# Token loop of a fused mixture-of-experts, two-attention and FFN kernel: layer two's values and layer one's context ahead of both value halves

## The chip, the cores and the metric

One core of a Trainium2 chip runs the whole program. The metric is the device time in microseconds; the time before is the median of three runs. TensorE (PE) does the matmuls, with its weight loads (PEld) running beside them; VectorE (DVE), ScalarE (ACT), GpSimd (POOL) and SyncE (SP) each work through a queue of their own in the order in which the kernel writes them, and wait for one another by semaphores.

## The reference

A residual block over 32 sequences of 64 tokens with 256 channels:

```
x = x + attn1(experts(x, cond))          # 8 experts, top 2; 16 heads of 64, tanh projections, causal
x = x + ffn(attn2(x, cond))              # 16 heads of 16, coherence gate and field term; FP4 rounding

attn1: q, k, v = tanh(s @ W + b);  p = softmax(mask(q k^T / 8));  tanh((p v) @ Wo + bo)
attn2: q, k, v = x @ Wqkv^T + b;   mod = softmax(q k^T / 4) * coh / sum;
       mod = 0.79 * mod + 0.21 * field;  (mod v) @ Wout^T + bout
```

The weights come in float32 and so do nearly all matmuls; the FP4-rounded product at the end is done in bfloat16 parts.

## The kernel before

**Stages.** The program first computes the gate, sorts the token slots by expert and runs the experts over 128-row tiles (up to some 320 us). Then a token loop takes the 2048 tokens as TT = 16 tiles of 128 tokens, two sequences each, through both attention layers and the FFN. The order of the work is written out by hand, one list of steps for each engine, and the loop is pipelined over tiles: in TensorE's turn t (lines 1080 to 1112) layer one works on tile t (projections, values, scores) and on tile t-1 (turning the probabilities, context, output projection), layer two on tile t-2 (projections, scores, values) and on tile t-3 (context, output, FFN). VectorE's list (lines 1916 to 1942) is the same pipeline with its index one higher: its turn t+1 serves TensorE's turn t.

**TensorE's steps around the change.** After the key projections of tile t come
- `l2_scores(t - 2)` (line 983, matmuls at L993): all heads' scores of layer two into banks 4 to 7;
- `l1_v(t, 0)` (line 860, L869): the values of the first sequence of tile t, 8 matmuls, into bank 3;
- `l1_context(t - 1)` (line 908, L919): layer one's context into banks 1 and 2;
- `l1_v(t, 1)`: the values of the second sequence, into bank 0;
- `l2_v(t - 2)` (line 971, L978): layer two's values into bank 6. It waits until both subtractions on VectorE have read the scores, which lie in banks 4 to 7:

```
pe.wait_ge(u2_set, 2 * t + 2)
```

- `l1_scores(t)` (line 874, L887): layer one's scores into banks 3 and 0, which hold the value halves until then, so it waits for both value biases (`vb_set`);
- `l2_turn_q(t - 3)` (L1033) and `l1_out(t - 1)` (line 923, L928), the output projection, which waits for the two context copies.

The value halves are called value half 0 and 1 below. `tail_busy` puts small matmuls on bank 0 in single turns after the last tile.

**VectorE's steps around the change.** `l2_max` (line 1829, L1834) takes the row maxima of layer two's scores in two halves, `l2_shift` (line 1836, L1840) subtracts them, in two halves, and each subtraction releases one exponential of 512 columns on ScalarE (`l2_exp`, L1323). `l1_v(t, s)` (line 1752, L1758) adds the value bias to a half and moves it from PSUM to `v`; for half 0 it also waits for the context of the tile before, since that reads `v`:

```
dve.wait_ge(v_ps, 2 * t + s + 1)
if t and s == 0:
    dve.wait_ge(ctx_ps, t)
```

`l1_ctx` (line 1778, L1783) copies the context out of PSUM, in two halves. `l2_sums` (line 1850, L1854 to L1857) are four instructions, the row sums of both exponentials and what is made of them. `l2_v` (line 1815, L1824) adds layer two's value bias, two instructions, after `v2_ps`. `l2_share` (line 1859, L1862) then scales the exponentials. Later in the turn come the mask (L1765), the bias of the output projection (L1790) and more.

**Other queues.** GpSimd gathers the expert outputs of a coming tile, SyncE loads x and stores the result; ScalarE does tanh, exponentials and copies out of PSUM in its own list (from line 1361).

Of the kernel before, what the change touches and what calls it, by code (L numbers as in the profile page):

```python
# [30 lines left out]
TT = TOK // P  # L31
# [64 lines left out]
def exists(t, n):  # L96

    return not isinstance(t, int) or 0 <= t < n
# [12 lines left out]
def value_bank(t, s):  # L111

    return (1, 2)[s] if t == 0 else (3, 0)[s]
# [46 lines left out]
def build(nc, t_in, out):  # L160
    ctx = ExitStack()
    with ctx:
# [453 lines left out]
        def _(pe):  # L616
# [205 lines left out]
            def halves():  # L822

                return [(s, slice(s * SEQ, (s + 1) * SEQ)) for s in range(2)]

            def l1_turn_m(t):
                if not exists(t, TT):
                    return
                pe.wait_ge(m_set, t + 1)
                if t > 1:  # L830
                    pe.wait_ge(exp1_set, 2 * t)
                elif t == 0:
                    pe.wait_ge(h1t_set, SLOT_TILES)
                for k in range(KH):
                    last = pe.transpose(ps[:, turn_bank(t), k * P:(k + 1) * P], m_rows[:, k * P:(k + 1) * P], ident[:, :])
                last.then_inc(mt_ps, 1)
# [23 lines left out]
            def l1_v(t, s):  # L860
                if not exists(t, TT):
                    return
                if t:
                    pe.wait_ge(qk_set, 4 * t + 3 + s)
                if t == 1:
                    pe.wait_ge(exp1_set, 1 + s)
                for k in range(KH):
                    for r in range(2):
                        last = mm(ps[r * SEQ:(r + 1) * SEQ, value_bank(t, s), :], m_t[:, k, s * SEQ:(s + 1) * SEQ],  # L869
                                  wv[:, k, r * 512:(r + 1) * 512], start=k == 0, stop=k == KH - 1,  # L870
                                  tile_position=(0, r * SEQ))
                last.then_inc(v_ps, 1)
# [35 lines left out]
            def l1_context(t):  # L908
                if not exists(t, TT):
                    return  # L910
                pe.wait_ge(pt1_set, 2 * t + 2)
                pe.wait_ge(v_set, t + 1)
                for cm in range(4):
                    for s, q in halves():
                        for r in range(2):
                            rows_ = slice(r * SEQ, (r + 1) * SEQ)
                            for g in range(2):
                                at, h = cm * P + s * SEQ, 2 * cm + g
                                last = mm(ps[g * D1:(g + 1) * D1, 1 + r, at:at + SEQ], v[rows_, s, h * D1:(h + 1) * D1],  # L919
                                          pt1[rows_, 4 * g + cm, q], start=True, stop=True, tile_position=(r * SEQ, g * D1))  # L920
                last.then_inc(ctx_ps, 1)
# [49 lines left out]
            def l2_v(t):  # L971
                if not exists(t, TT):
                    return
                pe.wait_ge(u2_set, 2 * t + 2)
                for s, q in halves():
                    for k in range(KH):
                        for r in range(2):
                            last = mm(ps[r * SEQ:(r + 1) * SEQ, 6, s * P:(s + 1) * P], x1_t[:, k, q],  # L978
                                      wv2[:, k, r * P:(r + 1) * P], start=k == 0, stop=k == KH - 1,
                                      tile_position=(0, r * SEQ))  # L980
                last.then_inc(v2_ps, 1)
# [54 lines left out]
            def l2_ffn(t):  # L1036
                if not exists(t, TT):
                    return
                pe.wait_ge(xqt_set, t + 1)
                for k in range(KH):  # L1040
                    for n in range(PARTS):
                        last = mm(bank(7, HID), xq_t[:, k, :], wffn[:, k, n, :], start=k + n == 0,
                                  stop=(k, n) == (KH - 1, PARTS - 1))
                last.then_inc(f_ps, 1)

            def tail_busy(t, last, n):
                if t == last:
                    for _ in range(n):
                        mm(bank(0, P), ident_h[:, :], ident_h[:, :], start=True, stop=True)
# [30 lines left out]
            for t in range(2, TT + 4):  # L1080
                l1_turn_m(t)
                l2_ffn(t - 4)
                tail_busy(t, TT + 2, 20)
                l2_turn_p(t - 3, 0)
                l1_q(t, 0)
                l2_turn_p(t - 3, 1)
                l1_turn_x1(t - 2)
                l1_q(t, 1)
                l2_hidden(t - 2)
                l2_context(t - 3)  # L1090
                l1_k(t, 0)
                l2_coherence(t - 2)
                l2_out(t - 3)
                l2_q_or_k(t - 2, 4, wq2)
                l1_turn_p(t - 1, 0)
                l2_q_or_k(t - 2, 5, wk2)
                l1_k(t, 1)
                l1_turn_p(t - 1, 1)
                tail_busy(t, TT, 14)
                tail_busy(t, TT + 1, 20)  # L1100
                l2_scores(t - 2)
                l1_v(t, 0)
                tail_busy(t, TT, 12)
                l1_context(t - 1)
                l1_v(t, 1)
                tail_busy(t, TT, 10)
                tail_busy(t, TT + 1, 44)
                l2_v(t - 2)
                l1_scores(t)
                tail_busy(t, TT + 2, 70)  # L1110
                l2_turn_q(t - 3)
                l1_out(t - 1)
# [272 lines left out]
        def _(dve):  # L1385
# [366 lines left out]
            def l1_v(t, s):  # L1752
                if not exists(t, TT):
                    return
# [3 lines that stand above are left out]
                tt(v[:, s, :], bank(value_bank(t, s)), half_row("bv"), ALU.add).then_inc(vb_set, 1)  # L1758
# [19 lines left out]
            def l1_ctx(t, n):  # L1778
                if not exists(t, TT):
                    return  # L1780
                if n == 0:
                    dve.wait_ge(ctx_ps, t + 1)
                dve.tensor_copy(ctx_t[:, 4 * n:4 * n + 4, :], ps[:, 1 + n, :].rearrange("p (c q) -> p c q", c=4)  # L1783
                                ).then_inc(ctx_set, 1)
# [30 lines left out]
            def l2_v(t):  # L1815
                if not exists(t, TT):
                    return
                if t == 0:
                    dve.wait_ge(v2_zeroed, 1)
                dve.wait_ge(v2_ps, t + 1)  # L1820
                for s in range(2):
                    dst = v2[:, s, :, :].rearrange("p (g o) (w d) -> p g (o w) d", o=2, w=2)[:, :, 0::3, :]
                    src = lambda ap: ap.rearrange("p (g o d) -> p g o d", o=2, d=D2)
                    last = tt(dst, src(ps[:, 6, s * P:(s + 1) * P]), src(half_row("bv2")), ALU.add)  # L1824
                    last.then_inc(v2_set, 1)
# [24 lines left out]
            def l2_sums(t):  # L1850
                if not exists(t, TT):
                    return
                dve.wait_ge(exp2_set, 2 * t + 2)
                step(red(z2, u2, X, ALU.add))  # L1854
                step(stt(r2, coh, MOD_EPS, z2, ALU.add, ALU.mult))
                step(dve.reciprocal(r2, r2))
                step(stt(r2, coh, 1.0 - FI, r2, ALU.mult, ALU.mult))  # L1857
# [58 lines left out]
            for t in range(3, TT + 4):  # L1916
                l1_mix(t)
                l1_mask(t - 2, 1)
                l2_field(t - 4, 1)
                l1_sums(t - 2)  # L1920
                l1_share(t - 2)
                l2_bias_a(t - 4)
                l2_z(t - 3)
                l2_scales(t - 4)
                l2_coherence(t - 3)
                l2_round(t - 4)
                l2_max(t - 3, 0)
                l2_max(t - 3, 1)
                l2_shift(t - 3, 0)
                l1_v(t - 1, 0)  # L1930
                l2_shift(t - 3, 1)
                l1_ctx(t - 2, 0)
                l1_v(t - 1, 1)
                l1_ctx(t - 2, 1)
                l2_sums(t - 3)
                l2_v(t - 3)
                l2_share(t - 3)
                l1_mask(t - 1, 0)
                l1_bias_o(t - 2)
                l2_result(t - 4)  # L1940
                l2_x1_bias(t - 3)
                l1_residual(t - 2)
                l2_field(t - 3, 0)
# [72 lines left out]
```

## Time and profile before

| | |
|---|---|
| median of three runs | 769.49 us (768.01 to 771.59) |
| the profiled execution's own time | 771.83 us |
| its span in the trace | 770.1 us |
| granted clock of TensorE, mean | 0.986 |
| token loop at its full length, in the trace | 395 to 714 us |

Times in the trace are microseconds from the start of the span. "Idle before" is the time that an engine stood idle ahead of an instruction, with what released it ("<-"); a releaser of "issue" means that the profile shows nothing that was waited for. The ends of matmuls are modelled, and neighbouring matmuls overlap in the timeline; in the chain of waits the pieces are laid end to end. Some matmul records are missing (a piece of 64 is listed as x53).

### The profile page before, as it was taken

The numbers are of one execution on the slowest core, as the hardware profiler recorded it, in microseconds if no ns is written. First come the engines' busy times: TensorE is split into PE (matmuls) and PEld (weight loads), VectorE is DVE, ScalarE is ACT, GpSimd is POOL, SyncE is SP. The second block draws the span as 40 slices with busy tenths as digits, with TensorE's granted clock in tenths as the row PEclk, the third lists the DMA queues.
The fourth block names the chain that finished last, engine by engine and source line by source line (L and its number), as shares of the span: only waits on it lengthen the run. The fifth ranks groups of instructions, "written<-read, shape, count | busy, mean of one in ns | idle before, by whom it ended". The sixth has DMA issues, their size and how long they took to land.

```text
span 770.1 us, 22516 instructions
## 1 busy us (share of the span) xinstructions
PE 729.0 (95%) x9300; PEld 629.2 (82%) x9300; DVE 499.1 (65%) x1100; ACT 282.3 (37%) x823; POOL 87.9 (11%) x93
## 2 busy tenths in 40 slices
PE   5389999999999999989999999999999999999986
PEld 2279999569999999868888888897888889888775
DVE  3846564744454444244787778778777877877975
ACT  3032211141212212245445544544553555455331
POOL 2131112411111100111100110111011001000000
PEclk9599999999999999999999999999999999999999
DMA  7687411217111103200000010010010001000000
GB/s 261 259 328 264 152 35 52 81 48 254 42 35 36 38 19 111 90 29 22 22 17 15 29 30 9 23 29 23 9 30 29 16 16 29 17 2 16 16 9 14
DMA packets 20113, 49.26 MB, mean 64 GB/s; under 512 B 3051, under 2 KB 14699, under 8 KB 18477
## 3 DMA queue, kind: packets, MB, share of 16 engines
q1 hardware_dynamic: 10960, 32.47, 11.6%
q0 software_dynamic: 3744, 10.49, 4.7%
q10 hardware_dynamic: 5309, 4.87, 1.9%
q8 instruction: 74, 1.21, 0.7%
q14 instruction: 26, 0.21, 0.1%
HBM read 41.00 MB, written 6.82 MB: 62 GB/s over the span
## 4 chain that ended last, share of the span: by engine, by line
PE 90%; DVE 5%; ACT 2%; issue 1%; DMA 1%; another core or an unknown queue 0%; DVEq 0%; ACTq 0%; SPq 0%
PE ps L843 15%; PE ps L742 15%; PE ps L712 8%; PE ps L869 8%; PE ps L928 7%; PE ps L776 7%; PE ps L944 3%; PE ps L894 3%; PE ps L887 2%; PE ps L919 2%; PE ps L1025 2%; PE ps L959 2%; PE ps L1015 2%; PE ps L978 2%; PE ps L993 2%; PE ps L736 1%
## 5 line engine op out<-in xcount | busy, mean ns | idle before, releaser
L843 PE MATMUL ps<-arena,l_weights 128*128 128x128 f32 x1024 | 125.9, 277 | 2.1 <-issue 1.7
L742 PE MATMUL ps<-h_t,w_now 128*128 128x128 f32 x1056 | 123.5, 275 | 1.7 <-DVE h_t L1614 1.1
L843 PEld LDWEIGHTS ps<-arena,l_weights 128*128 128x128 f32 x1024 | 119.3, 192 | 4.1 <-issue 1.8
L742 PEld LDWEIGHTS ps<-h_t,w_now 128*128 128x128 f32 x1056 | 120.5, 192 | 2.1 <-issue 2.1
L1167 ACT ACTIVATE h_t<-ps,cols 128x128 f32<-128x128 f32 x132 | 37.6, 367 | 166.6 <-PE ps L712 144.4
L1589 DVE COPY w_now<-arena 128x2048 f32 x33 | 40.5, 1227 | 81.8 <-PE ps L742 75.3
L1240 ACT ACTIVATE arena<-ps,cols 128x128 f32<-128x128 f32 x256 | 73.6, 382 | 52.0 <-PE ps L843 52.0
L607 POOL DMA_INDIRECT arena<-expert_out,slot_of x32 | 32.7, 1023 | 333.9 <-DVE arena L1642 286.8
L712 PEld LDWEIGHTS ps<-xg_t,w_now 128*128 128x128 f32 x528 | 63.4, 192 | 5.7 <-issue 3.5
L712 PE MATMUL ps<-xg_t,w_now 128*128 128x128 f32 x528 | 65.0, 276 | 2.7 <-ACT h_t L1167 2.2
L576 POOL DMA_INDIRECT xg<-in_x,slot_tok x36 | 42.2, 1174 | 190.5 <-PE ps L691 159.2
L776 PE MATMUL ps<-arena,h_t 128*128 x264 | 62.5, 379 | 0.0
L869 PE MATMUL ps<-l_weights,arena 128*64 128x512 f32 x256 | 61.8, 604 | 0.0
L928 PE MATMUL ps<-l_weights,arena 128*128 128x256 f32 x256 | 58.9, 383 | 0.0
L928 PEld LDWEIGHTS ps<-l_weights,arena 128*128 128x128 f32 x256 | 47.4, 190 | 5.9
L776 PEld LDWEIGHTS ps<-arena,h_t 128*128 128x128 f32 x264 | 47.6, 190 | 5.1
L1574 DVE COPY w_now<-arena 128x1024 f32 x33 | 23.1, 701 | 31.4 <-PE ps L712 23.6
L1614 DVE TENSOR_SCALAR h_t<-ps,cols 128x128 f32<-128x128 f32 x132 | 37.0, 343 | 4.7 <-PE ps L742 4.6
L894 PE MATMUL ps<-ident,arena 128*128 128x128 f32 x256 | 38.4, 273 | 0.8 <-DVE arena L1862 0.6
L1758 DVE TENSOR_TENSOR arena<-ps,half_rows 128x512 f32<-128x512 f32 x32 | 22.0, 687 | 25.4 <-PE ps L919 19.9
L1878 DVE TENSOR_TENSOR arena<-ps,rows 128x256 f32<-128x256 f32 x16 | 6.8, 425 | 45.1 <-PE ps L1025 45.0
L1323 ACT ACTIVATE arena<-arena 128x512 f32<-128x512 f32 x32 | 20.1, 631 | 38.6 <-DVE arena L1840 38.6
(302 smaller groups left out, 1116.6 us busy)
## 6 DMA issues: line engine op xcount, KB each, us to landing
arena<-in_experts SPq DMA_DIRECT2D x8, 2048.0 KB
expert_out<-y ACTq DMA_DIRECT2D x36, 128.0 KB
arena<-in_x_t SPq DMA_DIRECT2D x2, 1024.0 KB, 7.5
arena<-in_x SPq DMA_DIRECT2D x16, 128.0 KB
out<-arena SPq DMA_DIRECT2D x16, 128.0 KB, 1.7
b<-in_b SPq DMA_DIRECT2D x1, 1024.0 KB, 5.0
l_weights<-in_wq SPq DMA_DIRECT2D x1, 1024.0 KB
l_weights<-in_wk SPq DMA_DIRECT2D x1, 1024.0 KB
```

The costliest lines, as they stand in the source:

```text
L576: pool.indirect_dma_start(out=xg[j % XG][:, :], out_offset=None, in_=t_in["x"], in_offset=bass.IndirectOffsetOnAxis(ap=slot_tok[:, slot_ti ...
L712: last = mm(ps[:, 0, m * P:(m + 1) * P], w1_now[:, k, m * P:(m + 1) * P], xg_t[:, k, :], start=k == 0, stop=k == KH - 1)
L742: last = mm(ps[:, 2, m * P:(m + 1) * P], w2_now[:, k, m * P:(m + 1) * P], h1_t[j % 2][:, k, :], start=k == 0, stop=k == KM - 1)
L776: last = mm(bank(4, HID), h2_t[j % 2][:, k, :], flat[:, bass.ds(at + k * HID, HID)], start=k == 0, stop=k == KM - 1)
L843: last = mm(ps[:, b, c * P:(c + 1) * P], wt[:, k, f:f + P], m_t[:, k, :], start=k == 0, stop=k == KH - 1)
L869: last = mm(ps[r * SEQ:(r + 1) * SEQ, value_bank(t, s), :], m_t[:, k, s * SEQ:(s + 1) * SEQ], wv[:, k, r * 512:(r + 1) * 512], start=k == ...
L894: last = pe.transpose(bank_[:, m * P:(m + 1) * P], p[:, h:h + 2, :], ident[:, :])
L928: last = mm(bank(1, HID), ctx_t[:, c, :], wo[:, c, :], start=c == 0, stop=c == C1 - 1)
L1167: last = f(h1_t[j % 2][:, k, :], ps[:, 0, k * P:(k + 1) * P], ACT.Relu, bias=cols[:, bass.ds(e * KM + at + k, 1)])
L1240: last = f(dst[:, cc, :], ps[:, project_bank(t, n), c * P:(c + 1) * P], ACT.Tanh, bias=col(bias)[:, cc:cc + 1])
L1589: dve.tensor_copy(w2_now[:, :, :].rearrange("p k n -> p (k n)"), arena[:, bass.ds(at, KM * MID)]).then_inc(w2_set, 1)
L1614: last = ts(h2_t[j % 2][:, k, :], ps[:, 2, k * P:(k + 1) * P], cols[:, bass.ds(e * KM + at + k, 1)], 0.0, ALU.add, ALU.max)
```

## The change

On TensorE, for the turns with t < 16, layer two's values move from behind the second value half to directly behind layer two's scores, and both value halves come after layer one's context, one behind the other. In later turns the order stays. On VectorE the bias of value half 0 leaves its place between the two subtractions; the two context copies and layer two's value biases come next, then the bias of half 0, the sums of layer two, and the bias of half 1.

```diff
@@ TensorE, turn t
                 l2_scores(t - 2)
-                l1_v(t, 0)
+                if t < TT:
+                    l2_v(t - 2)
                 tail_busy(t, TT, 12)
                 l1_context(t - 1)
+                l1_v(t, 0)
                 l1_v(t, 1)
-                tail_busy(t, TT, 10)
-                tail_busy(t, TT + 1, 44)
-                l2_v(t - 2)
+                if t >= TT:
+                    tail_busy(t, TT, 10)
+                    tail_busy(t, TT + 1, 44)
+                    l2_v(t - 2)
                 l1_scores(t)
@@ VectorE, turn t
                 l2_shift(t - 3, 0)
-                l1_v(t - 1, 0)
                 l2_shift(t - 3, 1)
                 l1_ctx(t - 2, 0)
+                l1_ctx(t - 2, 1)
+                l2_v(t - 3)
+                l1_v(t - 1, 0)
+                l2_sums(t - 3)
                 l1_v(t - 1, 1)
-                l1_ctx(t - 2, 1)
-                l2_sums(t - 3)
-                l2_v(t - 3)
                 l2_share(t - 3)
```

## Rows read from the trace of the kernel before

**Rows 1.** The page, part 1: engine, busy us, share of the span, instructions.

```profile
PE 729.0 (95%) x9300; PEld 629.2 (82%) x9300; DVE 499.1 (65%) x1100; ACT 282.3 (37%) x823; POOL 87.9 (11%) x93
```

**Rows 2.** Busy time by stretch, the full token loop: PE, PEld, DVE, ACT, POOL; clock, DMA, GB/s.

```profile
395.24:714.05 318.81, 318.74 (x5137) 270.30 (x5137) 248.62 (x527) 160.75 (x469) 20.97 (x20) 1.00 0.07 20
```

**Rows 3.** Chain of waits, start and length: L928 in turns 3 and 15.

```profile
395.24 3.51 PE ps L928 x16
...
714.05 3.51 PE ps L928 x16
```

**Rows 4.** Chain of waits, the changed stretch of turn 7.

```profile
493.82 0.84 PE ps L993 x53
494.66 1.87 PE ps L869 x8
496.53 1.09 PE ps L919 x64
497.62 1.87 PE ps L869 x8
499.49 0.87 PE ps L978 x16
```

**Rows 5.** Timeline of VectorE, the same stretch: start, length, instruction, idle before.

```profile
494.70 1.42 DVE L1834 TENSOR_REDUCE arena<-ps 128x8 f32<-128x512 f32 x2 [0.18 <-PE ps L993]
496.15 0.69 DVE L1840 TENSOR_TENSOR arena<-ps,arena 128x512 f32<-128x512 f32 x1
497.76 0.69 DVE L1758 TENSOR_TENSOR arena<-ps,half_rows 128x512 f32<-128x512 f32 x1 [0.92 <-PE ps L919]
498.37 0.68 DVE L1840 TENSOR_TENSOR arena<-ps,arena 128x512 f32<-128x512 f32 x1
498.96 0.68 DVE L1783 COPY arena<-ps 128x512 f32<-128x512 f32 x1
499.56 0.68 DVE L1758 TENSOR_TENSOR arena<-ps,half_rows 128x512 f32<-128x512 f32 x1
...
500.76 1.21 DVE L1854 TENSOR_REDUCE arena<-arena 128x16 f32<-128x1024 f32 x1
...
502.71 0.49 DVE L1824 TENSOR_TENSOR arena<-ps,half_rows 128x128 f32<-128x128 f32 x2
```

**Rows 6.** Timeline of the other engines, the same stretch.

```profile
499.08 0.63 ACT L1323 ACTIVATE arena<-arena 128x512 f32<-128x512 f32 x1 [1.58 <-DVE arena L1840]
499.10 1.02 PEld L978 LDWEIGHTS ps<-arena 128*64 128x64 f32 x16 [0.50 <-DVE arena L1840]
499.32 1.04 PE L978 MATMUL ps<-arena 128*64 128x128 f32 x16
...
500.30 1.02 PEld L887 LDWEIGHTS ps<-arena 64*64 64x64 f32 x64 [0.18 <-DVE arena L1758]
```

**Rows 7.** Timeline of the tail, turn 17.

```profile
752.28 1.09 PE L978 MATMUL ps<-arena 128*64 128x128 f32 x16 [1.01 <-DVE arena L1840]
752.92 1.22 DVE L1854 TENSOR_REDUCE arena<-arena 128x16 f32<-128x1024 f32 x1 [0.70 <-ACT arena L1323]
...
753.31 0.28 PE L1033 MATMUL ps<-before,arena 128*128 128x128 bf16 x2
...
754.88 0.49 DVE L1824 TENSOR_TENSOR arena<-ps,half_rows 128x128 f32<-128x128 f32 x2
755.29 1.22 DVE L1862 TENSOR_TENSOR arena<-arena 128x1024 f32<-128x1024 f32 x1
```

**Rows 8.** TensorE's idle times in the setup, and the clock by stretch.

```profile
7.86 1.93 PE L633 MATMUL ps<-arena 128*32 128x512 f32 x8 [3.48 <-DMA arena<-in_x_t]
...
21.82 0.29 PE L664 MATMUL ps<-maskb,before 128*128 128x128 bf16 x1 [5.71 <-DVE maskb L1465]
...
4.00:8.00 4.00, 0.52 (x8) 0.35 (x10) 1.87 (x12) 0.26 (x1) 1.26 (x5) 1.00 1.00 416
...
16.00:20.00 4.00, 0.10 (x1) 0.00 (x0) 3.41 (x14) 1.39 (x2) 0.00 (x0) 0.85 1.00 428
```

## Prediction, made before the change was run

> **What bounds the kernel now.** I began with the page's busy table: TensorE is busy for 95% of the span, VectorE for 65% [rows 1]. A share is an average, so the next view was the busy time of the stretch in which the token loop runs at its full length, 395.24 to 714.05 us: TensorE 318.74 of 318.81 us, granted clock 1.00, VectorE 248.62 [rows 2]. There TensorE has no idle time that anything could take away. The chain of waits gives the length of a turn: the attention output projection (L928) starts at 395.24 in one turn and at 714.05 twelve turns later [rows 3], 318.81 / 12 = 26.57 us a turn. So in this loop every wait of TensorE's queue, which runs in the written order, is new time, and no wait of another engine costs anything until TensorE stands behind it.
>
> Then I read one turn's chain from layer two's scores to layer one's scores [rows 4]. Scores of layer two end at 493.82 + 0.84 = 494.66; then value half 0 (1.87), context (1.09), value half 1 (1.87), layer two's values (0.87), done at 500.36, when layer one's scores follow. All the pieces touch. VectorE's timeline of the same stretch [rows 5] shows what these pieces cover: the two maxima start 0.04 after the scores, the first subtraction at 496.15, but the second only at 498.37, since the bias of value half 0 stands ahead of it and waits 0.92 for the context. Layer two's values on TensorE (L978) wait for the second subtraction: its weight load begins at 499.10, 0.05 after 498.37 + 0.68, while value half 1 is still streaming [rows 6]. The cover is just long enough. Layer one's scores (L887) wait for the bias of value half 1, which ends at 499.56 + 0.68 = 500.24; the load begins at 500.30 [rows 6]. That one is hidden by layer two's values.
>
> **The change part by part.** The work is the same, instruction for instruction: nothing is added or removed, no DMA moves, SP, POOL and ScalarE keep their order. Only what covers what changes, in the 14 turns t = 2 to 15 in which all the pieces exist.
>
> *Layer two's values directly behind layer two's scores (TensorE).* They write bank 6, which holds scores until both subtractions have read it, so l2_v waits for them, with only l2_scores ahead. That is a loop through VectorE that nothing can cover: maxima 494.70 + 1.42 = 496.12, first subtraction at 496.15, the second 0.60 later (the step between the PSUM readers of rows 5, as 498.37 to 498.96), 496.75 + 0.68 = 497.43, plus 0.05 to TensorE = 497.48. Queued behind the wait are the context, both value halves, layer one's scores and everything after. TensorE stands still 497.48 - 494.66 = **2.82 us**. The move on VectorE (bias of half 0 out from between the subtractions) is counted here: with the bias left there, each queue would wait for the other; so it is a condition of the first move and no saving on top.
>
> *What follows on TensorE.* Layer two's values, now from a standing start: in the tail they do this already, begun at 752.28 behind a wait, and the next piece begins at 753.31 [rows 7], so 1.03, done at 498.51. The low bound is the 0.87 of rows 4. Context 1.09: 499.60. Value halves 1.87 each: 501.47 and 503.34. Their inputs are ready: the pieces now come later than they did.
>
> *VectorE's order behind the subtractions.* Context copies wait for the context: 499.60 + 0.14 (before, the context ends at 496.53 + 1.09 = 497.62 and the bias starts at 497.76; the hand-over ahead of the maxima is 0.04) = 499.74, and the second 0.60 later, 500.34. Layer two's value biases from 500.94, 0.41 for both (754.88 to 755.29, [rows 7]): 501.35. Bias of half 0 waits for 501.47 + 0.14 = 501.61. Now **the piece the title does not mention**: l2_sums stands between the two biases. It needs the second exponential of layer two, 0.63 on ScalarE after the subtraction [rows 6], so about 498.2: ready. It starts 0.60 after the bias, 502.21, and its four instructions last 500.76 to 502.71 = 1.95 [rows 5], so 504.16. Bias of half 1: 504.16 to 504.85, although its product is there at 503.34. Layer one's scores may load at 504.85 + 0.06 = **504.91**; before, the load began at 500.30. TensorE's second stand is 504.91 - 503.34 = 1.57.
>
> *Per turn*: 504.91 - 500.30 = 4.61 (as a check: stands 2.82 + 1.57, restart 0.16, 0.06 from the pieces' start points). Times 14 = **64.5 us**. Bounds per turn: 4.2 (values at 0.87, no delay in the hand-overs) and 5.2 (each of the two restarts pays once more the 0.22 between load and first product, 499.10 to 499.32 in rows 6), so 59 to 73 us.
>
> *Who else is late.* Between layer one's scores and the next l2_scores both queues are unchanged. VectorE comes earlier to the attention shares of layer two (they follow the bias of half 1 directly; before, 2.8 after the score load), ScalarE's exponentials follow the scores as before, and VectorE waited for TensorE just ahead of the maxima. I cost all that at nothing; its cover is the 3.51 us of L928 [rows 3].
>
> *Tail, t = 16 and on.* The guard leaves TensorE's order as it was. VectorE takes layer two's value biases ahead of its sums there too. At t = 17 the sums started at 752.92; now the biases wait for L978, which ends at 753.37, so start 753.5, end 753.9, sums to 753.9 + 1.96 (752.92 to 754.88) = 755.9 against a share start of 755.29 [rows 7]: **+0.6 us**, on the chain. At t = 16 the projection covers the same delay: 0, bounded by the same 0.6.
>
> **Sum.** 64.5 + 0.6 = 65.1 us; 771.83 of the profiled execution (its span is 770.1) gives 836.9. That execution lies 2.3 above the median of the runs, 769.49, so on the median I forecast 834.6.
>
> **The clock.** A stand in every turn could cost clock. The rows: TensorE idle for 3.48 us ahead of the gate's products kept the granted clock at 1.00 (2.4 GHz) in 4 to 8 us; idle for 5.71 it shows 0.85 in 16 to 20 [rows 8]. The stands of 2.82 and 1.57 with 5.9 us of work between are shorter than the one that cost nothing. I take no loss.
> [...]
>
> **Rivals.**
> (a) *The clock falls in each turn.* For it: two stands a turn, 14 times, where rows 2 has none. Against it: rows 8. Price: if 4 us after a stand run at 1.2 GHz, 2 us of work are lost per turn, 28 us: 863.
> (b) *The second stand is shorter.* If the bias of half 1 were not behind the sums, it would end at 503.34 + 0.14 + 0.69 = 504.17 and the load begin at 504.23: 3.93 a turn, 55 + 0.6 us, 825. Only if sums finish before value half 1 does, that is if VectorE gains 0.7 us on rows 5. The order written in the diff speaks against.
> (c) *Faster.* The loop is really bound by the ring through VectorE (context, bias of half 0, second subtraction, values), and TensorE's records, whose ends are modelled, only look dense. Place: the 0.92 us wait ahead of the bias of half 0 [rows 5]; it goes. 14 x 0.92 = 12.9 us: 756.6. It decides only if TensorE could run its 5.7 us between the two scores in under 4.8; that the same pieces have the same length in every turn and load early (rows 6) speaks against.
> (d) *No change*: the two value halves side by side would have to save 4.6 us a turn, but last 3.74 together [rows 4]. Excluded as a single cause.
>
> **How the numbers follow.** Forecast 0.85 (834.6, own range 828 to 843 from the bounds 59 to 73); (b) 0.06; (a) 0.06, of which part is a smaller loss between the two; (c) 0.02; (d) 0.01. The range 825 to 848 takes in (b) and a partial (a), and leaves out the full (a), (c), (d). A measurement of this kernel can tell about 0.5% from no change: slower 0.97, same 0.01, faster 0.02.
>
> **What would show it.** Right: turn length 31.2 us between starts of L928; TensorE idle ahead of L978 of about 2.8 us with the second subtraction named as releaser, 14 times, and ahead of L887 of about 1.6 with the value bias named; the second subtraction 0.60 behind the first; the bias of half 1 directly behind the sums; granted clock 1.00 through the loop. Wrong: no idle ahead of L978, or a granted clock under 1.00 in the loop with matmuls of double length (a), or the idle ahead of L887 under 1 us (b), or new idle ahead of other lines than these two.

## The result, and the profile after

The changed kernel takes 860.03 us (median of six runs, 855.16 to 861.96) against 769.97 us of the kernel before (six runs): a ratio of 1.1165, with a 95% interval of 1.1132 to 1.1197. That is slower, as forecast, but by 90.1 us where 65.1 were forecast, and outside the range of 825 to 848. One of the four executions of the kernel with only its second stand filled (below) was in a slow state, 1192.71 us at a mean clock of 0.619; its ratio leaves that one out, and its median would be 851.01 without it.

A stand is, here as in the prediction, a stretch in which TensorE has nothing to do because the head of its queue waits.

The page of the profiled execution (span 853.4 us), busy time, the slices of TensorE and its granted clock, and a group of part 5:

```profile
PE 751.6 (88%) x9300; PEld 643.4 (75%) x9300; DVE 501.6 (59%) x1100; ACT 281.9 (33%) x823; POOL 87.9 (10%) x93
...
PE   4499999999999999897897897897988978978886
...
PEclk8699999999999999999999898999988999989999
...
L978 PE MATMUL ps<-arena 128*64 128x128 f32 x256 | 24.6, 353 | 40.7 <-DVE arena L1843 40.7
```

Two things differ from [rows 1]. TensorE's share fell from 95 to 88%, and its busy time rose, 729.0 to 751.6, with the same 9300 matmuls. A wait cannot do the second. The clock's row gives it away: 8 in several slices of the loop, where the kernel before has 9 throughout. (The changed kernel's VectorE lines are three higher: L1840 is L1843, L1834 L1837, L1758 L1761, L1783 L1786, L1824 L1827, L1854 L1857, L1862 L1865.)

Busy time of the twelve turns 4 to 15, from L928 to L928 as in [rows 2]:

```profile
400.56:796.78 396.22, 342.60 (x5138) 285.37 (x5137) 250.81 (x526) 160.33 (x468) 20.96 (x20) 0.93 0.06 16
```

396.22 / 12 = 33.0 us a turn against 26.57. TensorE is idle for 53.6 us of it, 4.47 a turn; and it is busy for 342.60 instead of 318.74, 23.9 us more, at a mean clock of 0.93.

The first stretch below is turn 3, which ran at full clock, the second turn 7, the turn of [rows 4] (timeline of TensorE: start, length, instruction, idle before):

```profile
391.94 1.09 PE L978 MATMUL ps<-arena 128*64 128x128 f32 x16 [2.83 <-DVE arena L1843]
392.96 1.16 PE L919 MATMUL ps<-arena 64*64 64x64 f32 x64
394.06 3.65 PE L869 MATMUL ps<-l_weights,arena 128*64 128x512 f32 x16
399.35 1.16 PE L887 MATMUL ps<-arena 64*64 64x64 f32 x64 [1.64 <-DVE arena L1761]
...
520.82 1.98 PE L978 MATMUL ps<-arena 128*64 128x128 f32 x16 [2.83 <-DVE arena L1843]
522.73 1.99 PE L919 MATMUL ps<-arena 64*64 64x64 f32 x64
524.64 4.83 PE L869 MATMUL ps<-l_weights,arena 128*64 128x512 f32 x16
531.11 1.16 PE L887 MATMUL ps<-arena 64*64 64x64 f32 x64 [1.63 <-DVE arena L1761]
```

Both stands are there, 2.83 and 1.64 us, in either turn. In turn 7 the work behind the first stand also takes longer, 1.98 for 1.09, 1.99 for 1.16 and 4.83 for 3.65. The clock over the same turn (columns as in [rows 2]; the stretches are the stand, the values with the context, the value halves, the second stand):

```profile
517.90:520.82 2.92, 0.09 (x9) 0.00 (x1) 2.67 (x4) 2.13 (x7) 0.00 (x0) 0.90 0.00 0
520.82:524.64 3.82, 3.82 (x80) 3.37 (x80) 0.00 (x0) 0.61 (x2) 0.00 (x0) 0.50 0.02 4
524.64:529.47 4.83, 4.83 (x20) 1.33 (x16) 3.35 (x6) 0.00 (x0) 0.00 (x0) 0.75 0.00 0
529.47:531.10 1.63, 0.00 (x1) 0.00 (x0) 1.49 (x6) 0.00 (x0) 0.00 (x0) 1.00 0.00 0
```

The granted clock falls to 0.50 (1.2 GHz) some 0.6 us before the stand ends (a mean of 0.90 over its 2.92 us), and returns to 1.00 (2.4 GHz) in the middle of the value halves. The fall does not always come inside the stand. In turn 5 the stand and layer two's values behind it (454.21 to 455.31) still have 1.00, and the clock falls as the context begins:

```profile
455.31:457.08 1.77, 1.77 (x65) 1.65 (x65) 0.00 (x0) 0.00 (x0) 0.00 (x0) 0.52 0.03 9
```

VectorE's timeline of turn 7, to set beside [rows 5]:

```profile
518.03 1.42 DVE L1837 TENSOR_REDUCE arena<-ps 128x8 f32<-128x512 f32 x2 [0.17 <-PE ps L993]
519.48 1.29 DVE L1843 TENSOR_TENSOR arena<-ps,arena 128x512 f32<-128x512 f32 x2
524.78 1.29 DVE L1786 COPY arena<-ps 128x512 f32<-128x512 f32 x2 [4.02 <-PE ps L919]
525.99 0.48 DVE L1827 TENSOR_TENSOR arena<-ps,half_rows 128x128 f32<-128x128 f32 x2
527.80 0.69 DVE L1761 TENSOR_TENSOR arena<-ps,half_rows 128x512 f32<-128x512 f32 x1 [1.34 <-PE ps L869]
528.41 1.21 DVE L1857 TENSOR_REDUCE arena<-arena 128x16 f32<-128x1024 f32 x1
...
530.36 0.69 DVE L1761 TENSOR_TENSOR arena<-ps,half_rows 128x512 f32<-128x512 f32 x1
```

The subtractions follow each other at once, and the sums stand between the two biases, as read off the diff.

**Where the 90 us went.** The starts of L928 give each turn's length. At full clock turn 4 is 31.13 us against 26.60 before, so the waits are 4.53 a turn; the first two turns give 4.67 and 4.60. Over 14 turns that is 4.67 + 4.60 + 12 x 4.53 = 63.6 us. From L928 of turn 1 to L928 of turn 15 the two traces differ by 455.10 - 368.43 = 86.7 us, which leaves 23.1 us. All of it lies in the 11 turns from 5 on, which are 32.4 to 34.0 us long: one fall costs from 1.2 to 2.9 us. The tail is 0.4 longer (56.62 against 56.21). The stretch ahead of the loop, which the change does not touch, was 3.8 us shorter in this execution: 86.7 + 0.4 - 3.8 = 83.3, the difference of the two spans. The medians differ by more, 90.1, also because this execution of the changed kernel was the fastest of its six (855.16 us at a mean clock of 0.955; the two slowest, 861.89 and 861.96, had 0.945).

### The profile page after: what moved, and what is told of

Its sections match the earlier page's. It is cut to its first block, busy times and chain, and to the rows that moved or that the text cites. A ratio compares the mean times of both kernels' runs of the same rounds, so it can differ in the third digit from the quotient of the medians.

```text
span 853.4 us, 22515 instructions
## 1 busy us (share of the span) xinstructions
PE 751.6 (88%) x9300; PEld 643.4 (75%) x9300; DVE 501.6 (59%) x1100; ACT 281.9 (33%) x823; POOL 87.9 (10%) x93
## 4 chain that ended last, share of the span: by engine, by line
PE 80%; DVE 15%; issue 2%; ACT 1%; DMA 1%; DVEq 1%; another core or an unknown queue 0%; SPq 0%; ACTq 0%
PE ps L843 14%; PE ps L742 13%; PE ps L712 7%; PE ps L928 7%; PE ps L776 6%; PE ps L869 5%; PE ps L944 3%; PE ps L919 3%; PE ps L894 3%; PE ps L978 3%; DVE arena L1837 2%; DVE arena L1761 2%; DVE arena L1843 2%; PE ps L887 2%; DVE arena L1857 2%; PE ps L1025 2%
## 5 line engine op out<-in xcount | busy, mean ns | idle before, releaser
L712 PE MATMUL ps<-xg_t,w_now 128*128 128x128 f32 x528 | 65.1, 276 | 2.9 <-ACT h_t L1170 2.2
L869 PE MATMUL ps<-l_weights,arena 128*64 128x512 f32 x256 | 66.9, 668 | 0.0
L1265 ACT ACTIVATE arena<-ps 128x512 f32<-128x512 f32 x32 | 19.0, 605 | 144.5 <-PE ps L887 144.5
L978 PE MATMUL ps<-arena 128*64 128x128 f32 x256 | 24.6, 353 | 40.7 <-DVE arena L1843 40.7
L928 PE MATMUL ps<-l_weights,arena 128*128 128x256 f32 x256 | 58.9, 383 | 0.0
L928 PEld LDWEIGHTS ps<-l_weights,arena 128*128 128x128 f32 x256 | 47.4, 190 | 5.9
L978 PEld LDWEIGHTS ps<-arena 128*64 128x64 f32 x256 | 19.4, 180 | 42.9 <-DVE arena L1843 42.8
L1786 DVE COPY arena<-ps 128x512 f32<-128x512 f32 x32 | 20.7, 685 | 47.1 <-PE ps L919 47.1
L869 PEld LDWEIGHTS ps<-l_weights,arena 128*64 128x64 f32 x256 | 18.7, 154 | 34.9 <-issue 33.3
L887 PEld LDWEIGHTS ps<-arena 64*64 64x64 f32 x1024 | 16.4, 134 | 37.7 <-DVE arena L1761 36.9
```

The lines of the kernel that those rows point to most:

```text
L712: last = mm(ps[:, 0, m * P:(m + 1) * P], w1_now[:, k, m * P:(m + 1) * P], xg_t[:, k, :], start=k == 0, stop=k == KH - 1)
L887: last = mm(slot(S1, 8 * g + 2 * cm + r)[q, :], q_t[rows_, c, q], k_t[rows_, c, q], start=True, stop=True, tile_position=(g * D1, s * SEQ))
L928: last = mm(bank(1, HID), ctx_t[:, c, :], wo[:, c, :], start=c == 0, stop=c == C1 - 1)
```

## The experiments

Each time stands beside runs of the kernel before in the same series on the same chip, since that kernel itself took 766 us in some series and 770 to 771 in others, and both on one chip. The edits are to the changed kernel, with two exceptions: the seven matmuls ahead of the context go into the kernel with the context first, and in the last section the edit is to the kernel with the values moved back. In the kernels with `fill` the lines of ScalarE and VectorE lie eleven higher than in the changed kernel: L1854 is there the subtraction (L1843) and L1772 the value bias (L1761).

### Filling the stands

`fill(t, b, n)` issues n matmuls `mm(bank(b, P), ident_h, ident_h)` in bfloat16, whose product nobody reads; the work of the kernel is unchanged. The first line below fills the first stand, the second line the second; each of the three kernels has the one, the other or both.

```diff
                 l2_scores(t - 2)
+                fill(t, 3, 40)
                 if t < TT:
                     l2_v(t - 2)
...
+                fill(t, 5, 22)
                 l1_scores(t)
```

The first stand alone:

> Forty small bfloat16 matmuls on bank 3 (free since the tanh of the first key half) stand between layer two's scores and layer two's values in every turn; nothing else differs from the changed kernel. The small matmuls fill about 2.4 us of the first stand of 2.83 us and add nothing to it. Theory A (the two stands cost 4.6 us a turn, and the rest of the loss, about 25 us of 90, is the clock that falls because TensorE is idle in the first stand): the granted clock is 1.00 through the loop, layer two's values, the context and the value halves take 1.09, 1.16 and 3.65 us in every turn, and the time is about 770 + 65 = 835 us. Rival B (those pieces are slow because VectorE and ScalarE work on PSUM beside them, or for another reason tied to the new order): they stay at up to 1.98, 1.99 and 4.83 us in most turns, and the time stays at 860.

Measured: 835.35 against 770.80 us, 1.0838 (1.0791 to 1.0884), so 64.6 us more. One turn of it (L1059 are the small matmuls), and twelve turns:

```profile
484.76 2.41 PE L1059 MATMUL ps<-before 128*128 128x128 bf16 x40
487.65 1.09 PE L978 MATMUL ps<-arena 128*64 128x128 f32 x16 [0.49 <-DVE arena L1854]
488.68 1.16 PE L919 MATMUL ps<-arena 64*64 64x64 f32 x64
489.77 3.65 PE L869 MATMUL ps<-l_weights,arena 128*64 128x512 f32 x16
495.06 1.16 PE L887 MATMUL ps<-arena 64*64 64x64 f32 x64 [1.63 <-DVE arena L1772]
...
402.84:776.07 373.23, 347.70 (x5618) 297.14 (x5617) 250.75 (x526) 160.35 (x468) 20.97 (x20) 1.00 0.06 18
```

The waits are as long as they were, 2.41 + 0.49 = 2.90 with the small matmuls in them; the clock is 1.00, the pieces have their full-speed length in all 14 turns, and 25.5 of the 90.1 us are gone (two series, each against its own runs of the kernel before). TensorE did more work and the kernel became faster than the changed one. Theory A held, rival B fell.

Both stands:

> As before this one, with 22 more small matmuls on bank 5 ahead of layer one's scores, which fill about 1.3 us of the second stand of 1.64 us. Theory A with the first stand alone as the cause of the clock's fall: the same time as with the first stand filled, 835 us. Theory A2 (both stands together matter): 835 here, but between 840 and 860 with only the first filled. Rival B: 860 in both.

835.13 against 770.80 us, 1.0830 (1.0801 to 1.0859): no different.

The second stand alone:

> The changed kernel with the 22 small matmuls on bank 5 ahead of layer one's scores alone: the second stand is filled, the first of 2.83 us is bare. Theory A (the first stand alone makes the clock fall): falls in most turns as in the changed kernel, 855 to 860 us. Rival A2 (the two stands only do it together): granted clock 1.00 and 835 us.

851.26 against 766.65 us, 1.1087 (1.1060 to 1.1114), so 84.6 more. The first stand stays at 2.83, and the clock falls in every one of the 14 turns; a turn is 32.3 to 32.5 us. So the first stand is enough to make the clock fall, and the second takes no part that filling it could remove. A fall costs less here, some 1.3 us (32.3 to 32.5 against 31.1 a turn with both stands filled): 14 falls are some 19 us against 23 for the changed kernel's 11, which is most of the 5 us beneath it.

Half of the first stand, 20 small matmuls:

> The changed kernel with 20 small matmuls in place of 40 in the first stand, so that about 1.7 us of it are idle. If the length of one idle stretch decides, this is like the stand of the kernel with the context first (1.23 behind 0.44), whose clock fell in every second turn: a value between 835 and 860, about 845. If what decides is idle time summed over both stands, it is worse than that. If 1.7 us are short enough: 835.

830.81 against 766.65 us, 1.0835 (1.0813 to 1.0858), so 64.2 more. Idle ahead of L978 is 1.61 us (1.68 in the first), the clock 1.00 in all. Neither 845 nor worse: this much idle time in one piece cost no clock, although the second stand of 1.63 us follows in each turn.

### One part of VectorE's order undone

```diff
                 l1_v(t - 1, 0)
-                l2_sums(t - 3)
                 l1_v(t - 1, 1)
+                l2_sums(t - 3)
```

> The changed kernel, but on VectorE the bias of value half 1 stands ahead of layer two's sums. Theory A: the second stand falls from 1.64 to about 0.9 us (0.14 + 0.69 + 0.06), the first stays at 2.83 and the clock goes on falling as in the changed kernel, so 14 x 0.74 = 10 us less, 850 us. If the second stand had a part in the clock's fall, less than 847. Rival C (the second stand is set by something else, such as the two value halves' own end): it stays at 1.64 and the time at 860.

849.12 against 770.80 us, 1.1024 (1.0991 to 1.1058): 78.3 more, so 11.7 less than the changed kernel. In the turn below, at a low clock, VectorE waits for the value halves ahead of both biases instead of doing the sums; the idle time of TensorE ahead of L887 is 0.8 us in all turns, and the clock falls in 13 of 14.

```profile
495.64 0.69 DVE L1761 TENSOR_TENSOR arena<-ps,half_rows 128x512 f32<-128x512 f32 x1 [1.19 <-PE ps L869]
497.35 0.69 DVE L1761 TENSOR_TENSOR arena<-ps,half_rows 128x512 f32<-128x512 f32 x1 [1.02 <-PE ps L869]
497.96 1.21 DVE L1857 TENSOR_REDUCE arena<-arena 128x16 f32<-128x1024 f32 x1
```

So the sums between the biases cost 0.84 us a turn, which the title of the change doesn't mention. Rival C fell.

### The context ahead of layer two's values

```diff
-                if t < TT:
-                    l2_v(t - 2)
                 tail_busy(t, TT, 12)
                 l1_context(t - 1)
+                if t < TT:
+                    l2_v(t - 2)
```

> The changed kernel, but TensorE does layer one's context between layer two's scores and layer two's values, so that the first stand shrinks to 2.83 - 1.09 = 1.74 us. VectorE's copies follow the subtractions at once. The bias of half 1 then ends some 1.1 us earlier: 3.5 us more a turn than the kernel before. Theory A with a clock that does not fall at stands this short: 770 + 49 = 819 us and a granted clock of 1.00. If it falls all the same: up to 844.

826.04 against 770.80 us, 1.0710 (1.0646 to 1.0775), so 55.2 more, between the two cases. One turn:

```profile
479.03 1.16 PE L919 MATMUL ps<-arena 64*64 64x64 f32 x64 [0.44 <-ACT arena L1271]
481.42 1.90 PE L978 MATMUL ps<-arena 128*64 128x128 f32 x16 [1.23 <-DVE arena L1843]
483.10 4.53 PE L869 MATMUL ps<-l_weights,arena 128*64 128x512 f32 x16
```

Two things were not foreseen. The context itself waits 0.44 us, for ScalarE's copy of the turned probabilities; value half 0 had covered that. And the clock falls in 5 of 14 turns, every second one from turn 6 on; a fall lengthens the turn from 29.90 to 31.6 us, 8.4 us in all. The four executions lie far apart, from 819.89 us at a mean clock of 0.983 to 829.29 at 0.973, so the number of falls seems to differ from one to the next; only one has a trace. Is it the 0.44 us, or that the work between is done in small tiles? Two kernels ask.

```diff
                 tail_busy(t, TT, 12)
+                fill(t, 3, 7)
                 l1_context(t - 1)
```

> The kernel with the context first, with 7 small bfloat16 matmuls in the 0.44 us ahead of the context, so that 1.23 us are the only idle time of the first stand. If the idle time (0.44 and 1.23) is what let the clock fall in every second turn: clock 1.00 and 826 - 10 = 816 us. If it is that scores and context are small tiles and the 1.23 idle us stand among them (theory F): falls remain, above 820.

813.15 against 766.58 us, 1.0599 (1.0569 to 1.0629), so 46.6 more, 8.6 less than without the seven matmuls. The wait of 1.24 stays, the clock is up in every turn:

```profile
476.93 0.56 PE L1059 MATMUL ps<-before 128*128 128x128 bf16 x7
477.44 1.16 PE L919 MATMUL ps<-arena 64*64 64x64 f32 x64
479.83 1.09 PE L978 MATMUL ps<-arena 128*64 128x128 f32 x16 [1.24 <-DVE arena L1854]
```

With seven matmuls of 0.08 us the five falls of 1.7 us are gone. Then small tiles in the first stand of the changed kernel, 80 float32 matmuls of 64x64 in place of the 40:

> The changed kernel with 80 float32 matmuls of 64x64 tiles (half of the array's rows) on bank 3 in the first stand, in place of 40 bfloat16 matmuls that use the whole array. Both fill about 2.3 us. Theory E (any matmul keeps the clock up): granted clock 1.00 through the loop and about 831 to 835 us. Theory F (small tiles hold the clock less than full ones): the clock falls in some turns although TensorE is not idle, 840 to 860 us.

859.32 against 766.58 us, 1.1194 (1.1160 to 1.1229). By its time this would be theory F; the trace says otherwise:

```profile
491.00 4.88 PE L1058 MATMUL ps<-ident 64*64 64x64 f32 x160
...
495.81 1.09 PE L978 MATMUL ps<-arena 128*64 128x128 f32 x16
...
406.00:799.00 393.00, 373.43 (x7010) 324.91 (x7011) 249.87 (x526) 159.21 (x468) 20.96 (x20) 1.00 0.06 17
```

My time for the filling was wrong by a factor of two: the 80 matmuls take 4.88 us, not 2.3, longer than the stand that they were to fill, and the turn is 32.83 us instead of 31.13; each is listed as two records, and they do not overlap as the 64 of the context do (1.16 us). But the clock is 1.00 throughout: in this trace matmuls of small tiles held it up as full ones did in the one above, in a stretch of 4.88 us. Theory E held for the clock, its time did not. So in the kernel with the context first the small tiles were not the cause, and the idle time was: 1.23 us with the 0.44 ahead of it, where 1.24 alone did nothing. Each side of this rests on one trace.

### The side-by-side halves without the stands

Layer two's values go back behind the halves on TensorE; VectorE does subtractions, context copies, both value biases, sums, layer two's value biases.

```diff
                 l2_scores(t - 2)
-                if t < TT:
-                    l2_v(t - 2)
...
                 l1_context(t - 1)
                 l1_v(t, 0)
                 l1_v(t, 1)
...
+                l2_v(t - 2)
                 l1_scores(t)
...
                 l1_ctx(t - 2, 1)
-                l2_v(t - 3)
                 l1_v(t - 1, 0)
-                l2_sums(t - 3)
                 l1_v(t - 1, 1)
+                l2_sums(t - 3)
+                l2_v(t - 3)
```

> Only the part of the change that adds no loop through VectorE: TensorE does layer two's scores, layer one's context, both value halves side by side, then layer two's values as in the kernel before; VectorE does both subtractions, both context copies, both value biases, then sums and layer two's value biases. Theory A: layer two's values find the subtractions done, and layer one's scores find the bias of half 1 done (1.09 + 3.65 + 0.14 + 0.69 + 0.06 = 5.63 us after the scores, against 5.61 of matmuls), so no stand and a turn of 26.6 us: the time of the kernel before, 768 to 771, clock 1.00. Rival D (the halves side by side, or the context ahead of them, cost something themselves): above 775.

770.72 against 765.84 us, 1.0071 (1.0055 to 1.0087), and in a second series:

> The order with layer two's values back behind the halves once more, beside the two that follow, to compare on one chip: 770 to 776, some 0 to 5 us above the kernel before.

770.82 against 766.05 us, 1.0059 (1.0041 to 1.0077). 85 of the 90 us are gone; the stands are gone, and what is left is the context's wait, seen here for the first time in a dense turn, with the halves behind it (they take 3.48 us from their start to the start of L978; before, half 0 took 1.87 and half 1 1.77, from 497.55 in TensorE's timeline to 499.32 in [rows 6]):

```profile
491.54 1.16 PE L919 MATMUL ps<-arena 64*64 64x64 f32 x64 [0.43 <-ACT arena L1268]
492.64 3.65 PE L869 MATMUL ps<-l_weights,arena 128*64 128x512 f32 x16
496.12 1.04 PE L978 MATMUL ps<-arena 128*64 128x128 f32 x16
497.09 1.16 PE L887 MATMUL ps<-arena 64*64 64x64 f32 x64
```

### A version faster than both

ScalarE reaches those copies late because the tanh of layer one's values stands ahead of them, while it idles for 1.06 us earlier in the turn. So the tanh moves there:

```diff
                 l1_k(t, 0)
+                l1_v(t - 1)
                 l2_q(t - 2)
                 l2_ez(t - 2)
                 l2_k(t - 2)
-                l1_v(t - 1)
                 l1_pt(t - 1, 0)
```

> The order with layer two's values back behind the halves, and on ScalarE the tanh of layer one's values (1.07 us) ahead of layer two's query copies, into an idle time of 1.06 us, instead of ahead of the copies of the turned probabilities. The order without it has TensorE idle for 0.43 us a turn ahead of the context, until ScalarE's second such copy. If that wait goes and nothing takes its place: 14 x 0.4 = 6 us less than that order, 1 us less than the kernel before. If layer one's scores wait for the bias of half 1 instead, or layer two's query copies come late: no gain.

762.51 against 766.65 us, 0.9950 (0.9934 to 0.9967). Again, on one chip with the two beside it:

> The same kernel as in the call before, beside the others on one chip: if the 0.43 us ahead of the context are the whole of what the new order of the halves costs, 1 us below to 1 us above the kernel before.

763.65 against 766.05 us, 0.9970 (0.9957 to 0.9983).

> The kernel before with ScalarE's tanh of layer one's values moved in the same way. There is no wait of TensorE for ScalarE in this order, so nothing to gain: within 0.3% of the kernel before, 0 us expected.

765.48 against 766.05 us, 0.9994 (0.9983 to 1.0006): the tanh's place alone is worth nothing that these runs can show. With the halves side by side the turn is 26.17 us, against 26.32 for this last kernel with the old order of the halves:

```profile
488.57 1.16 PE L919 MATMUL ps<-arena 64*64 64x64 f32 x64
489.66 3.65 PE L869 MATMUL ps<-l_weights,arena 128*64 128x512 f32 x16
493.14 1.04 PE L978 MATMUL ps<-arena 128*64 128x128 f32 x16
494.12 1.16 PE L887 MATMUL ps<-arena 64*64 64x64 f32 x64
```

So the idea of the change, the context first and the halves side by side, does bring something, 0.15 us a turn or 0.3 to 0.5% of the kernel, once nothing waits for it.

## Why the prediction was wrong

- *Dense loop, every wait is new time*: right. The two stands came with the releasers named, in all 14 turns.
- *First stand 2.82 us*: 2.83 measured. *Restart 1.03*: 391.94 to 392.96, 1.02. *Second stand 1.57*: 1.64, since the halves side by side end a little sooner than 2 x 1.87. *Per turn 4.61*: 4.53 at full clock, 63.6 us for 64.5. With the first stand filled and the clock up, the kernel lies 64.6 us above the one before, against a forecast of 65.1.
- *Tail 0.6*: 0.4. The biases now wait for L978 and the sums follow, as worked out.
- *The clock, "I take no loss"*: **this step failed**, by 25 us. It took [rows 8] to show that an idle time of 3.48 us had cost no clock at 2.4 GHz, and held the stands of 2.82 us against that. The row does not show it (below), and the same 2.83 us that left the clock up in turns 2 to 4 brought it down in turns 5 to 15. Even a sound row without a fall bounds little when the pattern comes 14 times and one length of idle time can go either way. Rival (a) named the mechanism and gave 863 us, 3 from the result. In part that is luck: it priced 14 falls at 2 us, 28 in all, where the trace has 11 falls of 1.2 to 2.9, 23.1 in all. Its chance of 0.06 was the error, and so was a range that ended beneath it. The Trainium skill ("TensorE: Matmul & The Clock Gate", section "HAM oscillation — how this bites in real kernels") tells of a matmul loop that waits for a DMA in each step and begins each next step at the lower clock. This trace agrees in kind: from turn 5 on each turn runs a part of its next pieces at 1.2 GHz, behind a stand of 2.83 us.
- *Rival (b)*: the order in the diff is what runs; moving the bias ahead of the sums shortens the stand to 0.80 (0.87 worked out) and saves 11.7 us (10.4 with 14 x 0.74). *Rival (c)*: TensorE's dense rows were real; a loop through VectorE did not bound the turn. *Rival (d)*: the halves side by side gain 0.15 us a turn, not 4.6.
- *Who else is late, "nothing"*: right for the changed kernel, but I did not see that value half 0 covered ScalarE's copies for the context by 0.44 us. Behind a stand of 2.83 it could not show.

**What [rows 8] really shows.** L633 runs twice, each time eight matmuls of one shape. In the kernel before, the eight behind the idle 3.48 us took 1.93 us [rows 8] and the eight at 12.03 us took 1.03; in the changed kernel's trace the first eight took 1.06 (first fence, kernel before; second fence, changed kernel):

```profile
12.03 1.03 PE L633 MATMUL ps<-arena 128*32 128x512 f32 x8
...
18.00:19.00 1.00, 0.00 (x0) 0.00 (x0) 0.90 (x4) 0.00 (x0) 0.00 (x0) 0.91 1.03 442
```

```profile
6.28 1.06 PE L633 MATMUL ps<-arena 128*32 128x512 f32 x8 [1.90 <-DMA arena<-in_x_t]
...
15.00:16.00 1.00, 0.00 (x0) 0.00 (x0) 0.90 (x4) 0.00 (x0) 0.00 (x0) 0.53 1.00 426
```

So TensorE ran at its lower clock behind the 3.48 us, whatever the clock column of 4 to 8 us says: this trace's first clock record stands at 12.0 us, and ahead of it the view prints 1.00. It ran there before the idle time too: the 24 bfloat16 matmuls that end at 4.17 us took 2.74 us, 0.11 each, against 0.06 for the forty of the same shape in the first stand. The row can't tell what 3.48 idle us cost at the higher clock. The longer idle stretch of the setup can: 5.7 us ahead of L664, the same in all 15 traces. It shows a mean of 0.85 in [rows 8] because the clock fell at 18.8 us, 2.7 us after TensorE's last matmul (16.1). In the changed kernel's trace it fell at 15.1, 1.8 us after it (13.3). Over the 15 traces the fall comes 1.8 to 3.7 us into that stretch. A stand of 2.83 us lies between the two.

## What to carry to other kernels

In a loop where one engine is busy all the time, price every wait twice: once by its length, and once by the work behind it at half the clock. Before moving a consumer directly behind its producer, look for the loop through another engine (here scores, maxima, subtraction, values) and leave enough independent work between to cover it; if there is none, a few small matmuls in the gap kept the clock here. Before a clock column is taken as evidence, look at the lengths of the matmuls in the same stretch: the eight of L633 took 1.93 us under a printed 1.00, and 1.03 at the higher clock. Look also at what the piece you move away had been covering, in both places.

## What the runs showed of the hardware

- A stand of 2.83 us in each turn brought the clock down in 11, 13 and 14 of 14 turns of three kernels; 1.61 us in one piece in none; 1.24 us in none, but 1.23 and 0.44 us on both sides of 1.16 us of work in 5 of 14. In the setup the clock fell 1.8 to 3.7 us into the idle stretch ahead of L664, differently in each of the 15 traces; an idle time of a length between these two can end with the clock up or down. What decides between these is not settled.
- Matmuls of 64x64 tiles held the clock at 1.00 through a stretch of 4.88 us in each turn, as those of the full array did through 2.41 us (one trace each, and a second for the latter).
- The same instructions of one group have two lengths: the 64 matmuls of layer two's context (L1015) take 1.16 us in one turn and 1.13 to 1.17 in nine more of the kernel before (first fence), 0.86 in its other turns, and 0.86 us in all turns of the kernel with the values moved back (second fence):

```profile
511.55 1.16 PE L1015 MATMUL ps<-arena 64*32 64x64 f32 x64
```

```profile
508.34 0.86 PE L1015 MATMUL ps<-arena 64*32 64x64 f32 x64
```

In the kernel before most turns are 26.61 us, but its last two full ones 26.33, and the kernel with ScalarE's tanh alone moved, whose TensorE list is the same, has 26.32 throughout; 14 x 0.29 = 4.1 us is about what the kernel before differs by between series (770.8 and 766.1; one chip had 770.8 in one series and 766.7 in another). Its cause stays open.
